# Merged value rows, a bias added on GpSimd, and three narrow products per tile in layer two

## The reference

```python
xn = layernorm(x)                                   # no weights
q, k, v = xn @ Wq.T + bq, ctx @ Wk.T + bk, ctx @ Wv.T + bv
scores = q @ k.T / sqrt(D)                          # per batch, 1024 x 154
attn = softmax(the 32 largest scores of each row)   # the others are left out
x = x + tanh(g_xattn) * ((attn @ v) @ Wo.T + bo)
xn = layernorm(x)
out = x + tanh(g_ffn) * (relu(xn @ W1 + b1) @ W2 + b2)
```

## Time and profile before

| | |
|---|---|
| runs | 253.76, 253.85, 253.93 us |
| profiled execution | 253.36 us |
| its span, first to last instruction | 251.3 us |
| TensorE busy | 246.8 us |
| VectorE busy | 187.0 us |
| GpSimd busy | 170.4 us |
| ScalarE busy | 135.9 us |
| granted TensorE clock, mean | 0.999 of full |

### The profile page before, as it was taken

The page is one execution under the profiler, slowest core; times in us unless marked ns, Lnnn a source line. Parts: engine busy times, 40 slices in busy tenths (PEclk is TensorE's granted clock), DMA queues, the critical chain, the costliest instruction groups (busy, mean ns, idle before and its releaser), DMA issues.

```text
span 251.3 us, 4726 instructions
## 1 busy us (share of the span) xinstructions
PE 246.8 (98%) x1470; PEld 216.9 (86%) x1470; DVE 187.0 (74%) x784; ACT 135.9 (54%) x292; POOL 170.4 (68%) x224
## 2 busy tenths in 40 slices
PE   8999999999999999999999999999999999999995
PEld 7867799999999988898889888898889888988884
DVE  3699999998998993689886988977556969332024
ACT  2579486576657476436660485526661485135720
POOL 3377988997977699674579567873869367745640
PEclk9999999999999999999999999999999999999999
DMA  7993011070301000109112400110011000100202
GB/s 206 379 416 148 0 25 27 1 278 17 125 4 42 0 4 0 42 5 323 52 42 86 126 1 3 42 43 3 0 43 42 3 1 4 39 3 0 83 0 83
DMA packets 6872, 17.21 MB, mean 68 GB/s; under 512 B 800, under 2 KB 2368, under 8 KB 6592
## 3 DMA queue, kind: packets, MB, share of 16 engines
q1 hardware_dynamic: 6848, 16.93, 19.1%
HBM read 12.44 MB, written 4.19 MB: 66 GB/s over the span
## 4 chain that ended last, share of the span: by engine, by line
PE 93%; DVE 5%; issue 1%; ACT 0%; DVEq 0%
PE y_ps L495 24%; PE z_ps L481 12%; PE z_ps L480 12%; PE z_ps L482 12%; PE y_ps L502 12%; PE sc_ps L406 6%; PE pt_ps L427 3%; PE att_ps L448 1%; PE att_ps L461 1%; PE att_ps L445 1%; PE att_ps L447 1%; PE att_ps L446 1%; PE y_ps L308 1%; PE pt_ps L461 1%; DVE picked L1234 1%; PE z_ps L315 1%
## 5 line engine op out<-in xcount | busy, mean ns | idle before, releaser
L1621 POOL TENSOR_TENSOR hid_lo<-hid,hid_hi 128x512 fp32r<-128x512 f32 (+1 forms) x80 | 85.3, 1078 | 50.9 <-ACT hid L960 50.5
L495 PE MATMUL y_ps<-w_both,hid_hi 128*128 128x512 f32 x256 | 83.4, 400 | 0.0
L959 ACT ACTIVATE hid_hi<-z_ps,small_in 128x512 fp32r<-128x512 f32 (+1 forms) x80 | 48.2, 603 | 49.0 <-PE z_ps L482 48.3
L480 PE MATMUL z_ps<-x2nt_hi,w_hi 128*128 128x512 f32 (+1 forms) x160 | 56.7, 354 | 0.0
L481 PE MATMUL z_ps<-x2nt_lo,w_hi 128*128 128x512 f32 (+1 forms) x160 | 55.6, 347 | 0.0
L482 PE MATMUL z_ps<-x2nt_hi,w_lo 128*128 128x512 f32 (+1 forms) x160 | 55.4, 346 | 0.0
L502 PEld LDWEIGHTS y_ps<-w_both,hid_lo 128*128 128x128 f32 x248 | 46.6, 188 | 9.2
L502 PE MATMUL y_ps<-w_both,hid_lo 128*128 128x256 f32 x248 | 52.2, 279 | 0.0
L1292 DVE SCALAR_TENSOR_TENSOR x<-y_ps,tanh_g,x 128x256 f32<-128x256 f32 x64 | 26.8, 477 | 33.4 <-PE y_ps L502 32.4
L960 ACT ACTIVATE hid<-z_ps,small_in 128x512 f32<-128x512 f32 (+1 forms) x80 | 47.9, 599 | 0.0
L495 PEld LDWEIGHTS y_ps<-w_both,hid_hi 128*128 128x128 f32 x256 | 42.7, 188 | 4.0 <-DVE x L1292 0.3
(11 more groups left out here) (147 smaller groups left out, 359.1 us busy)
## 6 DMA issues: line engine op xcount, KB each, us to landing
x_ring<-x SPq DMA_DIRECT2D x8, 512.0 KB, 6.0
out<-x SPq DMA_DIRECT2D x15, 256.0 KB, 2.0
xt_in<-x_t SPq DMA_DIRECT2D x7, 512.0 KB, 4.8
w_in<-w SPq DMA_DIRECT2D x2, 1024.0 KB, 10.5
wkq_in<-w_kq SPq DMA_DIRECT2D x1, 514.0 KB, 3.4
wvo_in<-w_vo SPq DMA_DIRECT2D x1, 513.0 KB, 6.6
xt_in<-x_t SPq DMA_DIRECT2D x2, 256.0 KB, 5.7
ctx_in<-ctx_t SPq DMA_DIRECT2D x1, 462.0 KB, 9.6
```

Of the source, the lines that this page charges most:

```text
L480: mm(dst, w1_hi[:, k, cols], hi[:, k, toks], start=k == 0, stop=False)
L495: last = mm(y_ps[t % 3][:], hid_hi[:, q % RING, tile_of_unit(g, j)], w2_both[:, c, :], start=c == 0, stop=c == KF - 1)
L959: func(hid_hi[:, q % RING, cols], z_ps[q % 2][:, cols], ACT.Relu, bias=b1[:, c:c + 1]).then_inc(hid_hi_made, 1)
L1621: nc.gpsimd.tensor_tensor(hid_lo[:, q % RING, cols], hid[:, q % FULL_RING, cols], hid_hi[:, q % RING, cols], ALU.subtract).then_inc(hid_lo ...
```

## The change

1. **Values.** values_of(5) and other_rest go. One tile rest_ctx holds 26 rows of each batch at partitions 0, 32, 64 and 96 of the product, values_of(1) makes them all, and move_rests takes its rows from there. The high half of batch 0's rest is copied twice by ScalarE (partitions 0 to 31 and 32 to 63); VectorE makes the low half (first_rest_to_lo), which GpSimd did.
2. **Output bias.** GpSimd adds bo to one row in add_wo; TensorE's product with bo goes.
3. **First load.** The query and key weights come in two loads of one contraction half each; fold_queries runs half by half.
4. **Layer two of groups 0 to 3** (JOINED = 4): hid_hi with the high half, hid_hi with the low half, and hid_lo with the high half, each of 256 columns, all into one 256-column sum; VectorE's output is one addition a tile.
5. **Order.** The lists of all five engines are rearranged. At the start: SyncE loads x 0 and w_vo ahead of ctx 0, x 1 before x transposed 0, and x 2 only after x 3, which waits for residual(0, 1). fold_values(0) goes ahead of make_keys, weigh_wo ahead of copy_keys, stats_x(1) to before the first scale_scores, scale_scores(0, 1) ahead of pt_to_lo(0, 0), GpSimd's prepare behind add_wo, rstd_x(0, 1) behind first_values_to_lo. Later calls move by a few places.

```diff
+JOINED = 4
+def halves_before(t):
+    return t - TILES * JOINED
...
-        vals_ps = [z_ps[0], z_ps[1], z_ps[0], z_ps[1], y_ps[2], y_ps[2]]
+        vals_ps = [z_ps[0], z_ps[1], z_ps[0], z_ps[1], y_ps[2]]
...
-            def load_kq():
-                sp.dma_start(wkq_in[:], w_kq).then_inc(kq_loaded, 16)
+            def load_kq(k):
+                sp.dma_start(wkq_in[:, k, :], w_kq[:, k, :]).then_inc(kq_loaded[k], 16)
...
-            load_kq()
+            load_kq(0)
+            load_kq(1)
+            load_x(0)
+            load_vo()
             load_ctx(0)
-            load_x(0)
+            load_x(1)
             load_first_xt()
+            load_small()
             load_second_xt()
-            load_vo()
-            load_small()
+            load_ctx(1)
             load_xt(1)
             load_w1()
-            load_ctx(1)
-            load_x(1)
             load_w2()
+            load_xt(2)
+            load_x(3)
             load_x(2)
-            load_xt(2)
             move_rests()
...
+            def fold_queries():
                 for k in range(KD):
+                    pe.wait_ge(kq_loaded[k], 16)
+                    for m in range(KD):
+                        product = mm(z_ps[m][:, 0:D + 1], wk[:, k, m * P:(m + 1) * P], wq_in[:, k, :], start=k == 0, stop=k == KD - 1)
...
-                pe.wait_ge(wo_bv_added, 1)
+                pe.wait_ge(wo_bv_added, 2)
                 pe.wait_ge(key_bias_made, 1)
-                mm(y_ps[0][:, 0:D], ones[:], wo_bv[:, 1, :], start=True, stop=False)
-                pe.wait_ge(small_loaded, 16)
-                mm(y_ps[0][:, 0:D], ones[0:1, :], bo[0:1, :], start=False, stop=True).then_inc(value_bias_ps_made, 1)
+                mm(y_ps[0][:, 0:D], ones[:], wo_bv[:, 1, :], start=True, stop=True).then_inc(value_bias_ps_made, 1)
...
+                rows = hid_hi[:, q % RING, tile_of_unit(g, j)]
+                if g < JOINED:
+                    mm(y_ps[t % 3][:, 0:D], rows, w2_hi[:, c, :], start=c == 0, stop=False)
+                    last = mm(y_ps[t % 3][:, 0:D], rows, w2_lo[:, c, :], start=False, stop=False)
+                else:
+                    last = mm(y_ps[t % 3][:], rows, w2_both[:, c, :], start=c == 0, stop=c == KF - 1)
...
+            def first_rest_to_lo():
+                dve.wait_ge(vals_hi_made, 2)
+                dve.wait_ge(vals_copied, 2)
+                nc.vector.tensor_tensor(vals_rest[64:96, 0, :], values[0:32, 1, :], vals_rest[0:32, 0, :],
+                                        ALU.subtract).then_inc(first_rest_lo_made, 1)
...
+                if g >= JOINED:
+                    for t in (first, first + 1):
+                        dve.wait_ge(ffn_made, t + 1)
+                        add_half(t, 1).then_inc(y_half_made, 1)
                 for t in (first, first + 1):
-                    dve.wait_ge(y_half_made, t + 1)
+                    if g < JOINED:
+                        dve.wait_ge(ffn_made, t + 1)
+                    else:
+                        dve.wait_ge(y_half_made, halves_before(t) + 1)
                     add_half(t, 0).then_inc(y_made, 1)
...
             def add_wo():
                 pool.wait_ge(wo_bv_made, KD)
                 nc.gpsimd.tensor_tensor(wo_bv[:, 1, :], wo_bv[:, 0, :], wo_bv[:, 1, :], ALU.add).then_inc(wo_bv_added, 1)
+                pool.wait_ge(wo_bv_added, 1)
+                pool.wait_ge(small_loaded, 16)
+                nc.gpsimd.tensor_tensor(wo_bv[0:1, 1, :], wo_bv[0:1, 1, :], bo[0:1, :], ALU.add).then_inc(wo_bv_added, 1)
+                pool.wait_ge(wo_bv_added, 2)
```

More of the change, by code:

```diff
@@ L606, in _ @@
-            transpose_picked(1, 1)
+            layer_one(0, 1, 5)
+            layer_one(0, 1, 6)
+            transpose_x2n(1, 0)
+            layer_two(0, 1, 0)
+            layer_two(0, 1, 1)
+            layer_two(0, 1, 2)
+            transpose_picked(1, 1)
+            layer_one(0, 1, 7)
+            layer_one(1, 0, 0)
+            layer_two(0, 1, 3)
+            attend(1, 1)
+            scores(2, 1)
+            layer_one(1, 0, 1)
+            layer_one(1, 0, 2)
             layer_two(0, 1, 4)
+            layer_one(1, 0, 3)
@@ L608, in _ @@
             layer_two(0, 1, 5)
-            layer_one(1, 0, 0)
-            layer_one(1, 0, 1)
-            attend(1, 1)
-            layer_one(1, 0, 2)
             layer_two(0, 1, 6)
+            transpose_x2n(1, 1)
+            layer_one(1, 0, 4)
             layer_two(0, 1, 7)
-            transpose_picked(2, 0)
-            layer_one(1, 0, 3)
-            layer_one(1, 0, 4)
-            scores(3, 0)
-            layer_two(1, 0, 0)
-            layer_two(1, 0, 1)
-            transpose_x2n(1, 1)
@@ L622, in _ @@
             layer_one(1, 0, 5)
             layer_one(1, 0, 6)
+            layer_two(1, 0, 0)
+            transpose_picked(2, 0)
+            scores(3, 0)
+            layer_one(1, 0, 7)
+            layer_one(1, 1, 0)
+            layer_two(1, 0, 1)
+            attend(2, 0)
             layer_two(1, 0, 2)
             layer_two(1, 0, 3)
-            layer_one(1, 0, 7)
-            layer_one(1, 1, 0)
-            attend(2, 0)
+            transpose_picked(2, 1)
             layer_two(1, 0, 4)
@@ L630, in _ @@
             layer_two(1, 0, 5)
+            layer_two(1, 0, 6)
             layer_one(1, 1, 1)
+            attend(2, 1)
             layer_one(1, 1, 2)
-            transpose_picked(2, 1)
-            layer_two(1, 0, 6)
+            layer_one(1, 1, 3)
+            scores(3, 1)
+            layer_one(1, 1, 4)
+            layer_one(1, 1, 5)
             layer_two(1, 0, 7)
-            layer_one(1, 1, 3)
-            layer_one(1, 1, 4)
-            attend(2, 1)
-            layer_one(1, 1, 5)
             transpose_x2n(2, 0)
+            transpose_x2n(2, 1)
@@ L1357, in _ @@
             pt_to_lo(0, 1)
-            stats_x(2)
+            scale_scores(1, 1)
+            topk_round(1, 0, 2)
             residual(0, 1)
-            topk_round(1, 0, 2)
             topk_round(1, 0, 3)
@@ L1428, in _ @@
             topk_round(4, 1, 3)
-            pick(4, 1)
-            pt_to_lo(4, 0)
-            output(2, 1)
-            stats_x(5)
-            pt_to_lo(4, 1)
-            stats_x(6)
-            residual(4, 0)
-            residual(4, 1)
-            output(3, 0)
             scale_scores(5, 0)
             topk_round(5, 0, 0)
-            x2nt_to_lo(4, 0)
-            x2nt_to_lo(4, 1)
-            scale_scores(5, 1)
+            pt_to_lo(4, 0)
+            pick(4, 1)
             topk_round(5, 0, 1)
@@ L1445, in _ @@
             topk_round(5, 0, 3)
+            residual(4, 0)
             pick(5, 0)
+            pt_to_lo(4, 1)
+            output(2, 1)
+            scale_scores(5, 1)
             topk_round(5, 1, 0)
+            stats_x(6)
+            residual(4, 1)
             topk_round(5, 1, 1)
@@ L1716, in _ @@
             rstd_x(6)
+            rstd_x(7)
+            add_b2(4, 1)
             hid_to_lo(4, 0, 0)
@@ L1733, in _ @@
             normalise_x2(6, 0)
+            add_b2(5, 1)
             hid_to_lo(5, 0, 3)
```

529 lines of the change are left out of this document (252 added, 277 removed).

## The result

The changed kernel takes 256.17 us (median of six runs, 255.59 to 256.98) against 253.81 (253.06 to 254.31) of the kernel before, run beside it: ratio 1.0098, 95% interval 1.0075 to 1.0121. It is slower by 2.4 us; 252.9 was forecast. Its profiled execution took 255.59, its span is 253.8, and its granted clock 0.993 over the whole.

What follows compares the result with a forecast made beforehand. TensorE, busy 98% of the span, was taken as the bound. Terms: -1.3 us at 40 us, +0.45 for 60 remaining layer-two calls, 0 after, -0.85 in sum: 252.5 profiled, 252.9 as a median; eight-in-ten range 251.5 to 254.4.

Steps and rivals of the forecast that it cites:

- Loads reordered: Start: ctx lands at 8.3, scores(0,0) begins 1.25 us late at 10.8, fold_values(0) moved ahead; net loss 0.4, wrong by 0.6 either way.
- VectorE's prologue: VectorE before attend(0,0): stats_x(1) gone, 1.6 us less there; pt_to_lo(0,0) ends about 20.3; pick(0,1) held again beside GpSimd.
- Merged rows and bias: TensorE before the first layer one: values_of(5) gone, full 1.39 us; value bias off TensorE, 0.72 us.
- both handshakes: TensorE meets pt_to_lo at attend(0,0) (20.4 against 20.3) and GpSimd's normalising at x2n's transposes (25.1 against 24.9); both just hold.
- Halved load: First weight load: both halves land before the queries' products at 4.18; 0, at worst 0.4 us more if the second is late.
- Three 256-column products: Layer two, groups 0 to 3: 64 calls change, one more product's start-up each; +0.5 us, from -0.6 to +1.0.
- One sum per tile: Layer two: 16 VectorE additions, 7.6 us, go from an engine not the bound; 0, gain up to 0.2 at a few pair changes.
- The reordered calls: Groups 1 to 7: TensorE's operands ready before their turn up to about 60 us; 0, range -0.3 to +1.5 us.
- Rival C: load_x(2) behind load_x(3) lands after 42.7, stats_x(2) holds VectorE 2 us, TensorE late: +1.15, 255.0 us; chance 0.15.
- Rival B: New start eats the gain: x_t half or GpSimd's rest rows late, 0.7 to 1 us given back, 253.8 us; chance 0.18.

Runs made afterwards that it cites:

- experiment 2: Changed kernel with VectorE's first_stats_x(0) put back behind both centre_queries: 253.91 us, ratio 1.0022 to the kernel before.
- experiment 5: experiment 2's kernel with layer two undone (JOINED = 0, wide products in all groups): 255.54 us, ratio 1.0076 to the kernel before.
- Experiment 1: Kernel before with one move alone, first_stats_x(0) ahead of centre_queries on VectorE, loads as they were: 256.73 us, ratio 1.012.
- experiment 3: Changed kernel with seven 128-column filler products, result unused, in TensorE's idle time ahead of fold_values(0): 254.62 us, ratio 1.0034 to the kernel before.
- experiment 12: Changed kernel with GpSimd's w1_to_lo(0) made to wait for VectorE's add_ctx(1): 256.25 us, ratio 1.0078 to the kernel before.
- experiment 7: Kernel before with merged value rows, output bias on GpSimd and halved first load; wide products, old orders but for ctx loads and rest rows earlier: 254.16 us, ratio 1.0028.
- experiment 8: Kernel before with the halved first load alone (two loads of 128 rows, queries' products k outer): 254.30 us, ratio 1.0018.
- experiment 9: experiment 2's kernel with more of the old start given back (ctx 0 ahead of x(0), fold_values(0) behind scores(0,0), prepare() first): 254.33 us, ratio 1.0021.
- experiment 4: Kernel before with layer two of groups 0 to 3 as three 256-column products and one sum per tile, old orders: 254.45 us, ratio 1.003.
- experiment 10: experiment 9's kernel with GpSimd's w1_to_lo(0) made to wait for VectorE's add_ctx(1): 253.88 us, ratio 1.0012 to the kernel before.
- experiment 6: Changed kernel with JOINED = 0 and the start's loads and calls in the old order (ctx of other batches earlier), halved load kept: 257.03 us, ratio 1.0126.
- experiment 11: experiment 6's kernel with GpSimd's w1_to_lo(0) made to wait for VectorE's add_ctx(1): 255.09 us, ratio 1.0056 to the kernel before.

## Why the prediction was wrong, step by step

**Loads reordered: the step that failed.** The prediction put scores(0,0) at 10.8, behind the first x_t half alone, and costed the reordering at "Net loss 0.4". The x_t half was late by little (it landed at 11.1). What was missed is in the order of VectorE's calls: first_stats_x(0) had moved ahead of centre_queries, so a load of 512 KB stood in front of the chain centring, mt, keys, scores. And the load came later than the prediction's own sum has it: 4.1 for the weights and 1.4 for 512 KB put x(0) at 5.5, ahead of the centring at 5.65, and w_vo at 6.9; they landed at 7.1 and 8.7. In the new order w_vo too holds TensorE, 0.38 us in experiment 2 and 1.84 in experiment 5, for which the prediction has no term. I walked VectorE's prologue for what had left it (stats_x(1)) and from the scores on, not for what its first call waits for. Centring came at 8.01 instead of 5.65. Experiment 1 shows this step alone, +3.0 us; experiment 2 shows it undone, −1.9.

**The price of the wait was not on the list.** A wait of TensorE was counted as its length. Here it was followed by records at the lower clock (0.62 from 8 to 12 us), and experiment 3 gives 1.5 us of the loss back while VectorE still waits for x(0). Of experiment 2's 1.9 that leaves 0.4 for the lateness itself, as an estimate: runs of one kernel with and without the fall differ by 2.0 us in experiment 12, 1.7 in experiment 2 and 0.4 to 0.9 in experiment 1.

**Merged rows and bias: "so the full 1.39 goes".** The work went, and in the old order the time stayed (experiment 7). Only where the order gives VectorE room does some of it arrive: in experiment 2 x2n(0,1) is 0.9 us early, of the forecast 1.3. The forecast had 0.72 + 1.39 of work less 0.8 of losses, so this part was near in size, and right in its remark that both handshakes just hold.

**Halved load: "I take 0", above 0.4.** Between 0 and 1.0 us (the interval of experiment 8), the likeliest 0.5. The prediction looked at TensorE's start, 4.18, which did not move, and was right that both halves have landed by then. It has no term for one more product, two records, ahead of what VectorE reads first, 0.43 us or more. The rest of the lateness in the trace of experiment 8 is TensorE's lower clock, whose cause stays open.

**VectorE's prologue.** pick(0,1) was slow again, as forecast, its two halves taking 1.00 and 0.84 us. The Trainium skill, GPSIMD Engine Reference, Specifications, says that the two engines share SBUF interfaces and that VectorE's instructions with two SBUF inputs contend there. Trace and rule agree, and the prediction looked for the wrong victim: it weighed first_rest_to_lo, 0.42 us in experiments 2 and 9, and not add_ctx(1), which took 2.59 us in experiment 9 and began 0.09 us ahead of GpSimd in the changed kernel.

**Three 256-column products: +0.5.** Right: +0.8 by the ratio of experiment 4 (interval 0.3 to 1.2), and 0.5 of it behind 41 us. One sum per tile: taken at 0, which fits the old order, where experiment 4 has products and sum together; in the new one the joined form as a whole is 1.0 us (the traces) to 1.4 us (the ratios) quicker than the wide form (experiments 2 and 5).

**The reordered calls: "I take 0", above 1.5.** From x2n(0,1) to the last matmul the kernel before takes 207.1 us, experiment 4 207.6, experiment 2 208.2, the changed kernel 208.1. So +0.5 to 0.6 us beyond the joined products, inside the bound but not nothing. With the wide products it is 209.3, 2.2 over the kernel before, of which one wait for a y bank is 0.88 (experiment 5). Which of the later calls cost it I have not separated; no single wait of TensorE above 0.2 us shows behind 46 us in the changed kernel.

**Rival C**, load_x(2) behind load_x(3): its condition was met, the load landed after VectorE had come to it; its price was not, since VectorE lost 0.33 us at 45.84, with no wait of TensorE behind it. Rival B had the right stretch, the start that eats the gain, and a wrong cause: 0.8 us were put on late loads.

The sum, as it should have been, on the last matmul: −0.9 at 40 us for the new start without the wrong call, +0.5 for the joined products, +0.6 for the order, which is experiment 2 (+0.2 in its trace, +0.4 in its median); and +2.2 for first_stats_x(0) with the clock it takes down, which is the change, +2.4.

None of the versions tried is shown to be faster than the kernel before. The nearest is experiment 10 (ratio 1.0012); the best single run of all, 252.27, was one of experiment 9 whose add_ctx(1) was presumably ahead of GpSimd, which its time suggests and no trace of that run shows.

## What to carry to other kernels

When a diff moves a call in an engine's queue, look first at what the call waits for, above all a load, and then at everything that stood behind its new place: a short call at the head of a queue holds the whole chain for as long as its operand is away. Price an idle stretch of TensorE early in a kernel at more than its length, and look at the granted clock of the window behind it. Work taken off the busiest engine gives nothing in a stretch where its waits already come from another one, so ask of each stretch, not of the kernel, what bounds it. And before a late matmul is put down to a load, look at when the load landed and at how long the records are.

## What the runs showed of the hardware

A VectorE product with two SBUF operands (128x462) took 0.70 us alone and 2.59 us when a GpSimd product of 128x1024 had begun 0.30 us ahead of it; begun 0.09 us ahead itself, VectorE took 0.70 and GpSimd 2.86 instead of 2.38. In these traces the one that starts first runs at its usual length and the other is held. In the kernels of experiments 6 and 9 the runs fell into two groups 2 us apart, and one cross-engine wait removed the spread (none of 18 runs with it, ten of 18 without); in experiment 11 it costs about 0.2 us (255.09 against the quick run's 254.86). How near the two starts are doesn't tell when this happens: the changed kernel and experiments 2 and 3 have the same 0.09 us in their traces, and in none of them do runs of the same clock fall into two groups. Where both began within 0.03 us, in three traces, VectorE's smaller product (128x154) was the one held, 0.92 us instead of 0.38, although its record begins first.

A wait of 1.55 us on TensorE, in the first 10 us of the kernel, came with a granted clock of 0.62 from 8 to 12 us; seven products of 128 columns put into it kept the clock at 1.00 there and made the kernel 1.5 us faster.

The clock at which TensorE starts is not the same from run to run, and the granted clock of the view doesn't show it in the first microseconds: the lengths of the records do. The same eight records of the queries' products, begun between 4.05 and 4.28 us, took 1.90 us in one trace (each record 378 to 383 ns) and 3.39 in another (most of them 635 ns).
